# Compressed interaction layers behind an embedding gather: rows seven times in DRAM, two low parts made by accumulating DMAs, 15 groups split instead of 14

## The reference, cut to what matters

```
e = stack(tbl_f[ids[:, f]] for f in 0..38)          # (512, 39, 16)
x0 = xk = e
for W, b in ((w0, b0), (w1, b1), (w2, b2)):
    z = relu(einsum('bhd,bkd,hks->bsd', x0, xk, W) + b)   # 128 channels s
    layers 0 and 1: xk = z[:, :64]; direct gets z[:, 64:]
    layer 2:        direct gets all of z
logit = sum over d of concat(direct)                # (512, 256)
h = relu([logit, dense_ctx] @ W_top1 + b_top1)
h = relu(h @ W_top2 + b_top2)
y = h @ W_top3
```

## Time and profile before

| | |
|---|---|
| profiled execution, its own time | 660.38 us |
| its span, first to last instruction | 658.6 us |
| median of the three timed runs | 660.35 us |
| PE (TensorE matmul) busy | 613.0 us (93%) |
| DVE (VectorE) busy | 546.7 us (83%) |
| POOL (GpSimd) busy | 536.2 us (81%) |
| ACT (ScalarE) busy | 410.6 us (62%) |
| DMA moved | 78.60 MB, 119 GB/s over the span |
| mean granted TensorE clock | 0.987 of 2.4 GHz |

### The profile page before, as it was taken

How to read it: one execution, slowest core, us unless ns; L and a number is a source line. 1 busy time by engine, 2 the same in 40 slices (tenths; PEclk the granted TensorE clock), 3 DMA queues, 4 the chain that set the end, 5 groups by cost and what they waited for, 6 DMA issues and landing times.

```text
span 658.6 us, 6385 instructions
## 1 busy us (share of the span) xinstructions
PE 613.0 (93%) x1996; PEld 378.3 (57%) x1996; DVE 546.7 (83%) x616; ACT 410.6 (62%) x553; POOL 536.2 (81%) x325
## 2 busy tenths in 40 slices
PE   0169899999999999999999999999999999999998
PEld 0026465666656566656666666666566666655563
DVE  1248699898989898998989898989989898969740
ACT  2025857676676758576766757586777667575622
POOL 6657899898989899998989998999989886747520
PEclk9998899999999999999999999999999999999899
DMA  6689794938374756749384747567494847420000
GB/s 220 136 191 187 160 172 98 180 73 184 89 147 109 139 104 132 148 101 179 71 165 107 146 100 140 114 126 154 95 180 75 162 110 134 96 46 1 0 0 0
DMA packets 53216, 78.60 MB, mean 119 GB/s; under 512 B 39081, under 2 KB 42025, under 8 KB 49891
## 3 DMA queue, kind: packets, MB, share of 16 engines
q1 hardware_dynamic: 47566, 75.11, 54.9%
q0 software_dynamic: 5120, 1.29, 2.0%
q10 hardware_dynamic: 496, 1.80, 1.1%
HBM read 76.23 MB, written 1.94 MB: 119 GB/s over the span
## 4 chain that ended last, share of the span: by engine, by line
PE 38%; POOL 38%; ACT 11%; issue 6%; DMA 4%; DVE 3%; SPq 1%; DVEq 0%; ACTq 0%
POOL low L361 29%; PE z L681 20%; PE z L698 9%; POOL gat L351 9%; ACT x L448 7%; PE z L713 6%; ACT high L428 2%; DMA spread<-x_rows 2%; DVE prod L591 2%; DMA gat<-table_dram,index 2%; ACT r L472 1%; DMA x_rows<-gat 1%; DVE base L626 1%; DVE low L634 1%; PE base L758 1%
## 5 line engine op out<-in xcount | busy, mean ns | idle before, releaser
L361 POOL TENSOR_TENSOR low<-prod,high 128x1024 fp32r<-128x1024 f32 (+2 forms) x160 | 380.7, 2399 | 58.8 <-ACT high L428 57.7
L591 DVE TENSOR_TENSOR prod<-spread,x 128x1024 f32<-128x1024 f32 (+1 forms) x256 | 307.6, 1212 | 38.7 <-ACT x L448 37.7
L681 PE MATMUL z<-prod,w_sb 128*128 128x512 f32 (+3 forms) x608 | 294.0, 604 | 36.9 <-DVE prod L572 32.4
L428 ACT ACTIVATE high<-prod 128x1024 fp32r<-128x1024 f32 (+2 forms) x160 | 167.7, 1058 | 116.9 <-DVE prod L591 98.4
L698 PE MATMUL z<-high,high_w_L 128*128 128x512 f32 (+1 forms) x448 | 205.9, 459 | 1.0 <-ACT high L438 1.0
L713 PE MATMUL z<-low,high_w_L 128*128 128x512 f32 (+1 forms) x448 | 182.6, 488 | 5.5 <-POOL low L361 3.5
L681 PEld LDWEIGHTS z<-prod,w_sb 128*128 128x128 f32 (+3 forms) x608 | 116.2, 192 | 124.0 <-issue 101.6
L351 POOL DMA_INDIRECT gat<-table_dram,index x160 | 154.7, 967 | 37.0 <-issue 35.3
L698 PE MATMUL z<-high,low_w_L 128*128 128x512 f32 (+1 forms) x448 | 179.0, 400 | 0.0
L448 ACT ACTIVATE x<-z,bias_sb 64x512 f32<-64x512 f32 (+1 forms) x186 | 120.2, 646 | 15.1 <-PE z L681 7.4
L713 PEld LDWEIGHTS z<-low,high_w_L 128*128 128x128 f32 (+1 forms) x448 | 82.8, 190 | 71.7 <-issue 45.8
(11 more groups left out here) (37 smaller groups left out, 62.4 us busy)
## 6 DMA issues: line engine op xcount, KB each, us to landing
spread<-x_rows SPq DMA_DIRECT2D x139, 192.0 KB, 13.5
spread<-x_rows SPq DMA_DIRECT2D x30, 546.0 KB
spread<-x_rows SPq DMA_DIRECT2D x47, 256.0 KB, 4.2
spread<-x_rows SPq DMA_DIRECT2D x15, 468.0 KB
x0base<-x_rows SPq DMA_DIRECT2D x47, 78.0 KB
gat<-table_dram,index POOLq DMA_INDIRECT x160, 5.6
x_rows<-gat SPq DMA_DIRECT2D x16, 72.0 KB, 2.2
wt_sb<-wt_dram SPq DMA_DIRECT2D x2, 512.0 KB, 19.0
```

The costliest lines, as they stand in the source:

```text
L361: pool.tensor_tensor(low[0:rows, h, 0:k, :], prod[0:rows, slot(c, kind, g), 0:k, :], high[0:rows, h, 0:k, :].bitcast(F32), ALU.subtract).t ...
L428: act.activation(high[0:rows, split_slot(c, kind, g), 0:k, :], prod[0:rows, slot(c, kind, g), 0:k, :], ACT.Copy).then_inc(high_ready, 1)
L591: dve.tensor_tensor(prod[0:rows, slot(c, kind, g), :, :], spread[0:rows, c % 2, g, :].unsqueeze(1).to_broadcast([rows, k, N]), x[0:rows, : ...
L681: last = pe.matmul(z[:, :], w[0:rows, at + j, :], prod[0:rows, slot(c, kind, g), j, :], start=g == 0 and j == 0, stop=closes and j == k - 1)
```

## The change

- The rows of a chunk lie in DRAM seven times (39 x 7 rows). SyncE stores the gathered rows twice (four DMAs), and a DRAM to DRAM DMA (`repeat_x0`) writes five more copies. Partition p of layers 1 and 2 now takes row (17 * (p // 8) + g) mod 39 in group g, so one DMA of 128 partitions in 16 blocks of 8 loads a piece, and one of 128 partitions loads layer 0's rows. These wait for the copies (`x0_copied`). The weights' rows are laid out to match; the last group of L1 and L2 has 128 rows, not 96.
- Group L2 3 is split too (15 split groups). The low parts of L2 3 and L1 3 are made neither by GpSimd nor by VectorE: ScalarE writes the negative of the rounded product to a new tile `added` (ring of 3), one place later in its list, and GpSimd issues a DMA from the product to `added` with accumulation (product minus high part). TensorE takes these low parts 6 places later (`DMA_PLACES`), L2 3 behind L1 3 and L1 3 behind L1 9.
- The low part of L2 5, formerly summed at the end of its stage, comes behind L1 0.
- Rings: products 9 (8), high and low parts 5 each and counted apart (4). A high slot of a DMA group is free when its high matmuls are done (`high_summed`), a product slot of one when the DMA has landed.
- The weights of the top MLP go into `spread0` after the last L0 products.

```diff
-RING = 8
-HRING = 4
+RING = 9
+HRING = 5
+DRING = 3
-SPLIT = {"L0": (1,), "L2": (0, 1, 2, 5, 6, 8), "L1": (1, 2, 3, 5, 6, 7, 9)}
+SPLIT = {"L0": (1,), "L2": (0, 1, 2, 3, 5, 6, 8), "L1": (1, 2, 3, 5, 6, 7, 9)}
+BY_DMA = (("L2", 3), ("L1", 3))
+ADD_PLACES = 1
+NEG_PLACES = 1
+DMA_PLACES = 6
+def place_of_low(c, kind, g):
+    last = NUMBER[c, kind, (G0 if kind == "L0" else G1) - 1] + (OVER if kind == "L1" and c >= 1 else 0)
+    return ORDER[min(NUMBER[c, kind, g] + (DMA_PLACES if (kind, g) in BY_DMA else 1), last) - 1]
...
+            def repeat_x0(c):
+                sp.wait_ge(x0_stored[c % 2], 64 * (c // 2 + 1))
+                row = x0_dram[c, 0:1, 0:1]
+                to = x0_dram[c, 2 * F:2 * F + 1, 0:1]
+                sp.dma_start(bass.AP(to.tensor, to.offset, [[N, F], [F * N, COPIES - 2], [1, N]]),
+                             bass.AP(row.tensor, row.offset, [[N, F], [0, COPIES - 2], [1, N]])
+                             ).then_inc(x0_copied[c % 2], 16)
...
+            def load_spread0(c):
+                sp.wait_ge(prod_done, PROD_NUMBER[c - 1, "L0", G0 - 1])
+                sp.wait_ge(x0_copied[c % 2], 16 * (c // 2 + 1))
+                row = x0_dram[c, 0:1, 0:1]
+                sp.dma_start(spread0[:, :, :].rearrange("p t n -> p (t n)"),
+                             bass.AP(row.tensor, row.offset, [[N, P], [1, T0 * N]])).then_inc(spread0_in, 16)
...
-                for q in qs:
-                    many = min(end, F - q * G1) - at
-                    row = x0_dram[c, q * G1 + at:q * G1 + at + 1, 0:1]
-                    src = bass.AP(row.tensor, row.offset, [[0, QUAD], [1, many * N]])
-                    sp.dma_start(spread[q * QUAD:(q + 1) * QUAD, c % 2, at:at + many, :].rearrange("p g n -> p (g n)"),
-                                 src).then_inc(spread_in[p][c % 2], 16)
+                row = x0_dram[c, at:at + 1, 0:1]
+                src = bass.AP(row.tensor, row.offset, [[STEP * N, P // BLOCK], [0, BLOCK], [1, (end - at) * N]])
+                sp.dma_start(spread[:, c % 2, at:end, :].rearrange("p g n -> p (g n)"), src
+                             ).then_inc(spread_in[p][c % 2], 16)
...
+            def add_low(c, kind, g):
+                pool.wait_ge(neg_ready, ADD_NUMBER[c, kind, g])
+                rows, k = shape_of(kind, g)
+                pool.dma_start(added[0:rows, add_slot(c, kind, g), 0:k, :].rearrange("p k n -> p (k n)"),
+                               prod[0:rows, slot(c, kind, g), 0:k, :].rearrange("p k n -> p (k n)"), accum_op=ALU.add
+                               ).then_inc(low_added[BY_DMA.index((kind, g))], 16)
...
+            def take_neg_high(c, kind, g):
+                n = ADD_NUMBER[c, kind, g]
+                if n > DRING:
+                    act.wait_ge(mm_done, DONE[ADDED[n - 1 - DRING]])
+                rows, k = shape_of(kind, g)
+                act.activation(added[0:rows, add_slot(c, kind, g), 0:k, :],
+                               prod[0:rows, slot(c, kind, g), 0:k, :], ACT.Copy, scale=-1.0).then_inc(neg_ready, 1)
...
                 if old in POOL_NUMBER:
                     dve.wait_ge(pool_low, POOL_NUMBER[old])
+                elif old in ADD_NUMBER:
+                    dve.wait_ge(low_added[BY_DMA.index(old[1:])], 16 * (old[0] + 1))
```

More of the change, by code:

```diff
@@ L25 @@
 GBUF = 3
+BLOCK = P // 16
+STEP = 17
+COPIES = 7
 DELTAS = (F + 1) // 2
@@ L74, in stages_of @@
     return out
[L77 to L87, removed]
 STAGES = [x for i in range(NCH + 1) for x in stages_of(i)]
@@ L99 @@
 PROD_NUMBER = {x: n + 1 for n, x in enumerate(RINGED)}
+def place_of_low(c, kind, g):
+    last = NUMBER[c, kind, (G0 if kind == "L0" else G1) - 1] + (OVER if kind == "L1" and c >= 1 else 0)
+    return ORDER[min(NUMBER[c, kind, g] + (DMA_PLACES if (kind, g) in BY_DMA else 1), last) - 1]
+LOWS_BEHIND = {x: [y for y in ORDER if y[2] in SPLIT[y[1]] and place_of_low(*y) == x] for x in ORDER}
+NEGS_BEHIND = {x: [y for y in ADDED if NUMBER[y] + NEG_PLACES == NUMBER[x]] for x in ORDER}
+ADDS_BEHIND = {x: [y for y in ADDED if NUMBER[y] + ADD_PLACES == NUMBER[x]] for x in ORDER}
+FINISH = [y for x in ORDER for y in ([x] if x[2] not in SPLIT[x[1]] else []) + LOWS_BEHIND[x]]
+DONE = {x: n + 1 for n, x in enumerate(FINISH)}
 def tiled_behind(c, kind, g, places):
@@ L180, in tower_kernel @@
         low = sb("low", [P, HRING, 2, N], F32R)
+        added = sb("added", [P, DRING, 2, N], F32R)
         r01 = sb("r01", [P, N])
@@ L214, in tower_kernel @@
         x0_stored = [sem(f"x0_stored{b}") for b in range(2)]
+        x0_copied = [sem(f"x0_copied{b}") for b in range(2)]
         base_in = sem("base_in")
@@ L225, in tower_kernel @@
         pool_low = sem("pool_low")
+        neg_ready = sem("neg_ready")
+        high_summed = sem("high_summed")
+        low_added = [sem(f"low_added_{k}_{g}") for k, g in BY_DMA]
         tile_prod = sem("tile_prod")
@@ L260, in store_x0 @@
[L260 to L263, removed]
+                for at in (0, F):
+                    first = x0_dram[c, at:at + 1, 0:1]
+                    sp.dma_start(bass.AP(first.tensor, first.offset, [[D, P], [FPT * N, full], [1, D]]),
+                                 gat[:, c % GBUF, 0:full, :]).then_inc(done, 16)
+                    tail = x0_dram[c, at + FPT * full:at + FPT * full + 1, 0:1]
+                    sp.dma_start(bass.AP(tail.tensor, tail.offset, [[D, LAST], [1, D]]),
+                                 gat[0:LAST, c % GBUF, full, :]).then_inc(done, 16)
@@ L268, in load_base, with load_first @@
                 if c >= 1:
                     sp.wait_ge(base_ready, c)
-                row = x0_dram[c, 0:1, 0:1]
                 for j in js:
+                    row = x0_dram[c, (F - j * T0) % F:(F - j * T0) % F + 1, 0:1]
                     sp.dma_start(x0base[j * F:(j + 1) * F, :], bass.AP(row.tensor, row.offset, [[N, F], [1, N]])
                                  ).then_inc(base_in, 16)
-            def load_spread0(c, at, end, done, js=range(DPT)):
-                if c >= 1:
-                    sp.wait_ge(prod_done, PROD_NUMBER[c - 1, "L0", G0 - 1])
+            def load_first(at, end, done, js):
+                row = x0_dram[0, at:at + 1, 0:1]
@@ L279, in load_spread0 @@
                 for j in js:
[L280 to L286, removed]
+                    sp.dma_start(spread0[j * F:(j + 1) * F, at:end, :].rearrange("p t n -> p (t n)"),
+                                 bass.AP(row.tensor, row.offset, [[N, F], [1, (end - at) * N]])).then_inc(done, 16)
@@ L377, in _ @@
                             take_low(c, kind, g)
+                        for x in ADDS_BEHIND[c, kind, g]:
+                            add_low(*x)
                         for _ in range(gathers_after(i, kind, g)):
@@ L396, in load_first @@
                 for n, (at, end) in enumerate(FIRST_CUTS):
[L397 to L400, removed]
+                    row = x0_dram[0, at:at + 1, 0:1]
+                    act.dma_start(spread0[j * F:(j + 1) * F, at:end, :].rearrange("p t n -> p (t n)"),
+                                  bass.AP(row.tensor, row.offset, [[N, F], [1, (end - at) * N]])
                                   ).then_inc(spread0_first[n], 16)
[L403 to L411, removed]
             def take_base(c):
@@ L518, in _ @@
                             take_tile_high(*tiled_behind(c, kind, g, 1), 1)
+                        for x in NEGS_BEHIND[c, kind, g]:
+                            take_neg_high(*x)
                         if i == 1 and kind == "L0" and g == 1:
@@ L631, in take_tile_low @@
                 dve.wait_ge(tile_high, 2 * (TILED_NUMBER[c, kind, g] - 1) + t + 1)
+                if t == 0 and LOW_NUMBER[c, kind, g] > HRING:
+                    dve.wait_ge(mm_done, DONE[LOWS[LOW_NUMBER[c, kind, g] - 1 - HRING]])
                 rows, _ = shape_of(kind, g)
                 h = split_slot(c, kind, g)
-                dve.tensor_tensor(low[0:rows, h, t, :], base[0:rows, :], high[0:rows, h, t, :].bitcast(F32),
+                dve.tensor_tensor(low[0:rows, low_slot(c, kind, g), t, :], base[0:rows, :], high[0:rows, h, t, :].bitcast(F32),
                                   ALU.subtract).then_inc(tile_low, 1)
@@ L697, in sum_high @@
                     for v in (high_w, low_w):
-                        pe.matmul(z[:, :], v[kind][0:rows, at + j, :], high[0:rows, h, j, :],
+                        last = pe.matmul(z[:, :], v[kind][0:rows, at + j, :], high[0:rows, h, j, :],
                                   start=g == 0 and j == 0 and v is high_w, stop=False)
+                if (c, kind, g) in ADD_NUMBER:
+                    last.then_inc(high_summed, 1)
             def sum_low(c, kind, g, closes):
@@ L705, in sum_low @@
                 rows, k = shape_of(kind, g)
-                h = split_slot(c, kind, g)
                 tiled = TILED_NUMBER.get((c, kind, g))
-                if not tiled:
-                    pe.wait_ge(pool_low, POOL_NUMBER[c, kind, g])
+                if (c, kind, g) in ADD_NUMBER:
```

(26 more changed lines are left out.)

115 lines of the change are left out of this document (62 added, 53 removed).

## The result

The changed kernel takes 714.92 us (median of 4 runs, 712.56 to 716.92), the kernel before 660.28: ratio 1.0861, 95% interval 1.0818 to 1.0903. It is slower by 8.6%; the forecast was 655 with a range up to 684. The profiled execution took 712.56 us, its span 710.4, 51.8 more than before. By the starts of layer 2's first relu on ScalarE (108.08 before, 114.33 now) 6.3 us of that are lost by then, and 47.5 in the 13 chunks after it.

The account below looks back on a forecast made before the run. PE and a loop through ACT and POOL were taken to bind; the POOL chain sets the new period, 36.05 us. 15 periods x 0.32 = 4.8 plus 1.0 at the start: 660.4 - 5.8 = 654.6, said as 655; range 648 to 684.

Parts of the forecast that it names:

- What bounds the kernel: Per chunk: PE and a loop over PE, ACT and POOL both bind, repeating every 36.37 us.
- c, the price of an issue on GpSimd: POOL's slot for issuing one accumulating DMA: 1.13 us, bounded at 0.5 and 2.6, taken from a gather's slot.
- 2c - 2.58: Change of the POOL chain per chunk in us, given issue price c; nothing is gained at c = 1.32.
- The place and the time left: L2 3's DMA, issued by 302.6, is due at its low part behind L1 3 on PE at 308.7: 6.1 us.
- L = 6 us: Landing time of L2 3's accumulating DMA, between 3.9 and 13.4 us; taken as 6, just in time; called the weakest step.
- The rival's price: L2 3's DMA lands late, PE waits behind L1 3: 683 us, or 715 to 760 with today's queue; chance 0.26.
- The price of a late us: Landing of L2 3's DMA: each us over 6.3 costs 1 us a chunk.
- The Trainium skill's rules: DMA queues take turns packet by packet and 512 KB takes 3.2 us: the add in time with 2 us to spare.
- Loads, end: Row loads in the middle of the run cost nothing; the top weights' later loading at the end costs 0.
- Start: VectorE's wait for layer 0's rows at the start shrinks: 1 us off, from 3 off to 2 on.

Follow-up runs that it names:

- before_relu_late: The kernel before with one constant changed: the third part of relu0 on ScalarE comes behind L2 5 instead of L2 3; 653.0 us, ratio 0.991.
- places12_ring11: The changed kernel with DMA_PLACES 12 instead of 6 and a ring of 11 products instead of 9; 663.41 us, ratio 1.0064 to the kernel before.
- hold_loads: The changed kernel, but SyncE asks for the next chunk's rows only when the DMA of L2 3 has landed; 691.83 us, ratio 1.0507 to the kernel before.
- rows_only: The changed kernel with its row copies, wide transfers and rings, but 14 split groups and no accumulating DMA; 658.02 us, ratio 0.9995 to the kernel before.
- after: The profile of the changed kernel itself, with the whole change; 714.92 us, ratio 1.0861 to the kernel before.

## Why the prediction was wrong

- **What bounds the kernel**: right. The loop that I read from the earlier trace rows was taken at its word by `before_relu_late`, and the period fell.
- **c, the price of an issue on GpSimd: mis-sized, and with it the gain.** The issue takes 972 ns in the mean beside a gather's 0.96, but its slot, from one issue to the next where two stand together, is 1.30 us (250.72 to 252.02), not 1.13. By the prediction's own 2c - 2.58 that makes +0.02 us a chunk where -0.32 was forecast. `places12_ring11`, in which nearly nobody waits for these DMAs, bears it out: GpSimd starts the low part of L1 5 at 278.12, 10.61 us after ScalarE's piece behind the copies of x1 (267.51). Before it was 10.55 (310.87 - 300.32), and 10.23 was forecast. So even with every DMA in time there would have been no gain to speak of.
- **The place and the time left**: right in substance. I counted 6.1 us from the end of the issue; from its start, as landings are counted in the earlier trace rows, it is 7.2, and the trace has 7.5 (243.80 to 251.3).
- **L = 6 us: the step that failed.** It was 12.8 and 7.4 in turn. The DMA's own time was right (3.9 to 5.4 forecast, 4.5 to 4.7 measured). Wrong was the time in the queue. I let the loads' rate double, had them start 3.5 us ahead of the issue (298 and 301.46) and then let the DMA share with one piece only. Measured, the rate went up to 395 GB/s only for layer 0's rows and to 220 for the pieces, and the copies moved the loads right up to the issue, 2.2 us ahead of it. The DMA stood for 4.2 us while SyncE's queue moved 1.38 MB, most of layer 0's rows, and then had under half of the engines' time. The nearest row, the gathers of 7.6 to 10.4 us in the earlier trace rows, was there and I went against it; I had written "10 or more" beside it. The rival's price for that, 715 to 760, begins at the result, and I left it out of the range; that it comes so near is in part luck, for it took every chunk as late and each late us at 1 us, and both were off.
- **The price of a late us**: mis-sized. I took 1 us of time for each. Behind a wait of 5.34 us PE's granted clock is 0.68, so a DMA that late cost 8.3 in two chunks; against this, only every second chunk was badly late.
- **The Trainium skill's rules.** I read turns packet by packet (the Trainium skill, DMA: Bandwidth & Descriptors, "Queues, rings and completion order") as short ones, which would have had the DMA in time. `hold_loads` with 4.7 and 11.7 us speaks against short turns for a 512 KB DMA, as the gather did: GpSimd's queue moves nothing for 4 us. The 43% of the engines' time that it has behind that would fit turns; how long one is no row shows. The same page of the Trainium skill ("Anatomy of one DMA") with 2.0 us plus bytes / 436 GB/s gives 3.2 us as an estimate; the trace has 4.5 us at the least. (Against the 6.1 us that I counted, 3.2 leaves 2.9 to spare, not 2.)
- **Loads, end**: right, no wait for rows in `rows_only`, and equal time.
- **Start**: I took 1.0 us off. In `rows_only` layer 2's first relu starts at 106.56 beside 108.08, 1.5 us earlier, in one profile of each; the medians don't tell it from none.

## What to carry to other kernels

A DMA that a full engine waits for has to be priced at the landing time of the nearest small DMA issued in the same stretch, with that stretch's loads in the queue, not at its own size. When an asynchronous step replaces a synchronous one, every use of its buffers falls due too: moving the consumer only moved the wait to the ring slot. And before adding an engine's work to free another, look whether one short piece on the loop that binds can simply go later: here that was one constant, and worth more than the whole change.

## What the runs showed of the hardware

- A DMA of 512 KB issued by GpSimd between on-chip tiles, accumulating, lands in 4.5 us with nothing ahead and in 11.7 to 13.0 us some 2 to 5 us behind 3.3 MB of loads on SyncE's queue. It then moves next to nothing for 4 us and has 43 to 45% of the engines' time for the next 6 (`after`, `hold_loads`).
- Accumulation added 0.39 us to the issue (972 against 581 ns). At like distances behind the loads it added at most 1.1 us to the landing, and in two pairs of three next to nothing.
- Loads from DRAM ran at 395 GB/s in the window of layer 0's rows, where partition p reads seven rows from row p on in one DMA, at 220 in that of the pieces, where 8 partitions read the same row, and at 186 where 32 did. The size of the reads differs too, and no run varied the sharing alone.
- PE's granted clock was 0.68 over the 9 us behind an idle stretch of 5.34 us, a mix of 1.2 and 2.4 GHz, and 1.00 before it.
